# A deformable-convolution kernel: the three parts of a sampling weight row are joined by TensorE, written by ScalarE, and sampling runs in two halves of one PSUM bank

## The reference

```
x = x + attention(norm(x))                    # L0: channel attention, 256 x 256 scores
x = x + dynamic_conv(norm(x))                 # L1: 3x3 kernels made from the image itself
x = x + pointwise(depthwise(norm(x)))         # L2
x = x + dcnv3(norm(x))                        # L3: deformable convolution
# dcnv3: 16 groups of 16 channels, 9 taps a pixel
loc    = pixel + tap + offset                 # offset and mask come from the image
sample = bilinear(in_proj(x), loc)            # four neighbours of each point
out    = out_proj(sum over taps of mask * sample)
```

## Time and profile before

| | us |
|---|---|
| median of 3 runs | 6136.41 (6131.53 to 6136.68) |
| the profiled execution | 6134.27 |
| its span | 6132.4 |
| VectorE busy | 5269.1 |
| TensorE busy (matmul) | 2854.9 |
| ScalarE busy | 1331.2 |
| granted TensorE clock, mean | 0.739 of full speed |

### The profile page before, as it was taken

How to read it: one execution, slowest core, us unless ns; L and a number is a source line. 1 busy time by engine, 2 the same in 40 slices (tenths; PEclk the granted TensorE clock), 3 DMA queues, 4 the chain that set the end, 5 groups by cost and what they waited for, 6 DMA issues and landing times.

```text
span 6132.4 us, 43325 instructions
## 1 busy us (share of the span) xinstructions
PE 2854.9 (47%) x15026; PEld 1623.8 (26%) x15026; DVE 5269.1 (86%) x6291; ACT 1331.2 (22%) x1441; POOL 422.2 (7%) x293
## 2 busy tenths in 40 slices
PE   4442454545345453543545445454544545445233
PEld 2221222223222222322222232222322232232122
DVE  5689899898988989898898989989899898989961
ACT  1311222222122211312221122222212221122210
POOL 0000100001010000100000010000101000010000
PEclk9676676877768777776868678686776878777666
DMA  8101323232322313332241322323232231332253
GB/s 382 50 22 40 99 77 92 69 122 53 91 79 76 113 54 97 99 86 80 68 121 51 91 90 81 101 69 105 71 89 79 77 112 49 96 102 78 83 142 105
DMA packets 619820, 558.08 MB, mean 91 GB/s; under 512 B 463760, under 2 KB 545680, under 8 KB 615632
## 3 DMA queue, kind: packets, MB, share of 16 engines
q1 hardware_dynamic: 615616, 547.85, 29.5%
q0 software_dynamic: 3984, 7.45, 0.5%
HBM read 279.33 MB, written 275.78 MB: 91 GB/s over the span
## 4 chain that ended last, share of the span: by engine, by line
DVE 72%; PE 13%; issue 6%; ACT 5%; POOL 1%; DMA 1%; SPq 1%; DVEq 0%; POOLq 0%; ACTq 0%
DVE spread L1114 9%; DVE partial L1104 9%; DVE spread L1104 6%; DVE qx L776 5%; DVE work L776 5%; DVE partial L1123 5%; DVE partial L1122 5%; DVE work L838 5%; DVE work L829 4%; PE ps L485 4%; PE ps L596 3%; DVE stats L747 2%; PE ps L666 2%; DVE work L889 2%; PE ps L655 1%
## 5 line engine op out<-in xcount | busy, mean ns | idle before, releaser
L553 PE MATMUL ps<-work,w2x 128*128 128x512 f32 x1152 | 558.0, 614 | 174.9 <-DVE work L829 163.8
L1114 DVE TENSOR_TENSOR spread<-spread,partial 128x1344 f32<-128x1344 f32 x384 | 625.2, 1628 | 13.3
L1104 DVE TENSOR_TENSOR partial<-haty,hatx 128x1344 f32<-128x1344 f32 x384 | 596.6, 1554 | 5.6
L1104 DVE TENSOR_TENSOR spread<-haty,hatx 128x1344 f32<-128x1344 f32 x288 | 447.6, 1554 | 77.0 <-ACT qx L1275 64.4
L666 PE MATMUL ps<-samp,wout 128*128 128x256 f32 x1024 | 316.2, 463 | 329.6 <-ACT samp L1347 310.2
L1238 ACT ACTIVATE xp<-x,small 128x1024 f32<-128x1024 f32 x128 | 152.4, 1239 | 1338.4 <-POOL small L1372 1338.4
L485 PE MATMUL ps<-qx,work 128*128 128x512 f32 x512 | 271.6, 690 | 313.1 <-DVE work L855 312.4
L829 DVE SCALAR_TENSOR_TENSOR work<-ps,cols,qx 128x512 f32<-128x512 f32 x576 | 403.2, 746 | 14.3 <-PE ps L553 5.5
L596 PE MATMUL ps<-wts,work 128*128 128x432 f32 x512 | 221.6, 598 | 383.8 <-ACT work L1320 383.8
L485 PE MATMUL ps<-xp,wts 128*128 128x512 f32 x640 | 339.1, 678 | 87.7 <-ACT xp L1238 59.2
L1122 DVE TENSOR_TENSOR partial<-spread 128x576 f32<-128x576 f32 x288 | 344.6, 1196 | 23.0 <-DVE spread L1114 0.4
(11 more groups left out here) (231 smaller groups left out, 4986.2 us busy)
## 6 DMA issues: line engine op xcount, KB each, us to landing
band<-taps_dram SPq DMA_DIRECT2D x512, 384.0 KB
taps_dram<-partial SPq DMA_DIRECT2D x1280, 48.0 KB
near<-img_dram SPq DMA_DIRECT2D x256, 128.0 KB
img_dram<-band SPq DMA_DIRECT2D x6, 4096.0 KB, 40.8
taps_dram<-band SPq DMA_DIRECT2D x6, 4096.0 KB, 86.9
om_now<-om SPq DMA_DIRECT2D x32, 576.0 KB, 9.1
om_dram<-om SPq DMA_DIRECT2D x32, 576.0 KB, 9.6
x<-x_in SPq DMA_DIRECT2D x16, 1024.0 KB, 10.2
```

Source lines behind the costliest of these rows:

```text
L553: pe.matmul(bank(4 + i % 4), w2x[:, half, tap, :], tr[:, h * HALF:(h + 1) * HALF], start=True, stop=True).then_inc(s_w, 1)
L1104: return build(vec.tensor_tensor(o, haty[:, :, 3 * i:3 * i + 3, :].rearrange("p e j a -> p j e a"), cells, ALU.mult))
L1114: done = build(vec.tensor_tensor(skew, skew, spare, ALU.add))
```

## The change

The products and their adds of a unit now go, not skewed, into one of two buffers of `spread`. VectorE starts a unit once the row two back is written (`s_wrow`), and its two joining adds are gone. TensorE adds the three parts in bank 1 by products with the identity: the middle part over 448 columns, the other two over 384 each, shifted against each other. ScalarE writes the row into the ring in two skewed copies: the first and the last vertical distance straight from `spread`, the seven between out of the bank. The ring has two slots, and the wait for a slot's DMAs is now ScalarE's. The steps are `SUM_AT` (1.6 behind the unit's building), 0.2 more for ScalarE and 0.4 more for SP.

A quarter is sampled in two halves of 32 products, both in bank 0. The second half waits until ScalarE has copied the first. There are no zero products any more, but for one at the very start. `SECOND_AT`, `EVICT_AT` and `PROJECT_AT` hold the steps, and the projection of quarter 0 moves from L1 + 4.6 to dyn + 1.5, its result from dyn + 1.1 to dyn + 3.1.

```diff
-RING = 3
+RING = 2
+SUM_AT = [at + 1.6 for at in BUILD_AT]
+TAPS_NEAR = [[i for i in range(3) if abs(u % D - R - (i - 1)) <= REACH] for u in range(UNITS)]
+BUILT = list(accumulate(2 * len(near) - 1 + (u % D == 0) for u, near in enumerate(TAPS_NEAR)))
 SAMPLE_AT = [STEP["L1"] + 1.1, STEP["L2"] + 2, STEP["L3"] + 2, STEP["om"] + 5]
-RESULT_AT = [STEP["dyn"] + 1.1, STEP["pw"], STEP["ln"] - 1, STEP["end"]]
+SECOND_AT = [STEP["L1"] + 6.5, STEP["L2"] + 3, STEP["L3"] + 3, STEP["om"] + 6]
+EVICT_AT = [(STEP["L1"] + 3.5, STEP["L1"] + 8.3), (STEP["L2"] + 3.1, STEP["L2"] + 4.5), (STEP["L3"] + 3.1, STEP["L3"] + 5.2),
+            (STEP["om"] + 5.6, STEP["om"] + 8)]
+PROJECT_AT = [STEP["dyn"] + 1.5, STEP["L2"] + 5.5, STEP["L3"] + 5.6, STEP["om"] + 8.5]
+RESULT_AT = [STEP["dyn"] + 3.1, STEP["pw"], STEP["ln"] - 1, STEP["end"]]
...
-        spread = sb("spread", [P, 3, D, HG])
+        spread = sb("spread", [P, 2, 3, E, HG])
...
-                wait(sp, s_s, 4 * n + quarter)
+                wait(sp, s_s, 2 * (4 * n + quarter))
...
-                    yield at + 4
+                    yield EVICT_AT[quarter][1] + 0.5
...
+            def rows_of_weights(n):
+                for u in range(UNITS):
+                    yield SUM_AT[u]
+                    at = n * UNITS + u
+                    pe.wait_ge(s_wb, n * BUILT[-1] + BUILT[u])
+                    wait(pe, s_wrow, at)
+                    parts = spread[:, at % 2, :, :, :].rearrange("p j e a -> p j (e a)")
+                    inner = (D - 2) * HG
+                    pe.matmul(bank(1, inner), ident, parts[:, 1, :], start=True, stop=False)
+                    pe.matmul(bank(1, inner - HG), ident, parts[:, 0, HG:E * HG], start=False, stop=False)
+                    pe.matmul(bank(1, inner - HG, HG), ident, parts[:, 2, 0:inner - HG], start=False, stop=True).then_inc(s_sum, 1)
...
+                    for part in range(2):
+                        yield (SAMPLE_AT, SECOND_AT)[part][quarter]
+                        wait(pe, s_samp, 2 * at + part)
...
+                    wait(ve, s_wrow, at - 1)
...
-                    done = multiply(near_i[0], skew)
+                    done = multiply(TAPS_NEAR[u][0], total)
...
-                    wait(ve, s_w2[r], 16 * YB * (at // RING))
-                    ve.wait_ge(s_wb, build(vec.tensor_tensor(o, parts[0], parts[1], ALU.add)))
-                    vec.tensor_tensor(o, o, parts[2], ALU.add).then_inc(s_wrow, 1)
-                    ve.wait_ge(s_wrow, at + 1)
...
-                wait(ac, s_wrow, n * UNITS + half * D)
+                wait(ac, s_wb, n * BUILT[-1] + (BUILT[D - 1] if half else 0))
...
+            def rows_of_weights(n):
+                for u in range(UNITS):
+                    yield SUM_AT[u] + 0.2
+                    at = n * UNITS + u
+                    r = at % RING
+                    wait(ac, s_w2[r], 16 * YB * (at // RING))
+                    ac.wait_ge(s_sum, at + 1)
+                    o, parts = ring[:, r, :], spread[:, at % 2, :, :, :]
+                    skew = [[RUN + 1, YI], [YI, G]]
+                    act.activation(bass.AP(o.tensor, o.offset, [list(o.ap[0]), [(D - 1) * RUN, 2]] + skew),
+                                   bass.AP(parts.tensor, parts.offset, [list(parts.ap[0]), [(3 * E - 1) * HG, 2], [G, YI], [1, G]]),
+                                   ACT.Copy)
+                    act.activation(bass.AP(o.tensor, o.offset + RUN, [list(o.ap[0]), [RUN, D - 2]] + skew),
+                                   bank(1, (D - 2) * HG).rearrange("p (d i g) -> p d i g", d=D - 2, i=YI), ACT.Copy).then_inc(s_wrow, 1)
...
+                    for part in range(2):
+                        yield EVICT_AT[quarter][part]
+                        ac.wait_ge(s_s, 2 * at + part + 1)
+                        wait(ac, s_o, at)
+                        act.activation(samp[:, 2 * part:2 * part + 2, :].rearrange("p g (b i x) -> p (g b) i x", b=QB, i=YI),
+                                       bank(0).rearrange("p (b x i) -> p b i x", b=4, i=YI), ACT.Copy).then_inc(s_samp, 1)
```

More of the change, by code:

```diff
@@ L1 @@
 from contextlib import ExitStack
-from itertools import count
+from itertools import accumulate, count
 import concourse.bass as bass
@@ L75, with merged @@
 SAMPLE_AT = [STEP["L1"] + 1.1, STEP["L2"] + 2, STEP["L3"] + 2, STEP["om"] + 5]
[L76 to L77 removed]
+SECOND_AT = [STEP["L1"] + 6.5, STEP["L2"] + 3, STEP["L3"] + 3, STEP["om"] + 6]
[3 more added lines that the diff above has]
+RESULT_AT = [STEP["dyn"] + 3.1, STEP["pw"], STEP["ln"] - 1, STEP["end"]]
+POINTERS_AT, PLACES_AT, VALUES_AT, TURNED_AT, MIXED_AT = (STEP["L0"] + i for i in (1.5, 4.5, 8.5, 9.5, 11.5))
+def merged(*streams):
+    at = [next(stream, END) for stream in streams]
+    while min(at) < END:
+        i = at.index(min(at))
+        yield at[i]
+        at[i] = next(streams[i], END)
 def weave(*streams):
@@ L640, in sample, with taps @@
+            def taps(n):
+                yield from merged(far_points(n), rows_of_weights(n))
             def sample(n):
                 for quarter in range(4):
-                    yield SAMPLE_AT[quarter]
                     at = 4 * n + quarter
-                    wait(pe, s_samp, at)
-                    for b in range(2):
-                        pe.matmul(bank(b), zeros[:, :], cst[:, 0:512], start=True, stop=False, skip_group_check=True)
-                    pe.wait_ge(s_bl, PHASE_LOADS * (at + 1))
@@ L648, in sample @@
-                    for gq in range(4):
-                        for j in range(JB):
-                            a, z = R if j == 0 else 0, SLOTS - R if j == JB - 1 else SLOTS
-                            for s in range(4):
-                                g = 4 * gq + s
-                                o = ps[s * 32:s * 32 + CG, gq // 2, gq % 2 * Q:(gq % 2 + 1) * Q]\
-                                    .rearrange("p (b x i) -> p b x i", b=QB, i=YI)[:, :, j * BW - R + a:j * BW - R + z, :]
-                                mm = pe.matmul(o, near[:, j, g * CG:(g + 1) * CG], band[:, :, j, a:z, g, :],
-                                               start=False, stop=(j == JB - 1), skip_group_check=True)
@@ L657, in sample @@
-                    mm.then_inc(s_s, 1)
-                    yield SAMPLE_AT[quarter] + 3.5
-                    pe.wait_ge(s_samp, at + 1)
+                    for part in range(2):
+                        yield (SAMPLE_AT, SECOND_AT)[part][quarter]
+                        wait(pe, s_samp, 2 * at + part)
+                        if at == 0 and part == 0:
+                            pe.matmul(bank(0), zeros[:, :], cst[:, 0:512], start=True, stop=True)
+                            pe.wait_ge(s_bl, PHASE_LOADS)
+                        elif part == 0:
+                            pe.wait_ge(s_bl, PHASE_LOADS * (at + 1))
+                        for c in range(2):
+                            for j in range(JB):
+                                a, z = R if j == 0 else 0, SLOTS - R if j == JB - 1 else SLOTS
+                                for s in range(4):
+                                    g = 8 * part + 4 * c + s
+                                    o = ps[s * 32:s * 32 + CG, 0, c * Q:(c + 1) * Q]\
+                                        .rearrange("p (b x i) -> p b x i", b=QB, i=YI)[:, :, j * BW - R + a:j * BW - R + z, :]
+                                    mm = pe.matmul(o, near[:, j, g * CG:(g + 1) * CG], band[:, :, j, a:z, g, :],
+                                                   start=(c == 0 and j == 0), stop=(j == JB - 1), skip_group_check=True)
+                        mm.then_inc(s_s, 1)
@@ L1098, in rows_of_weights @@
                         ve.wait_ge(s_hy, 2 * n + half + 1)
-                    near_i = [i for i in range(3) if abs(dx - (i - 1)) <= REACH]
+                    wait(ve, s_wrow, at - 1)
                     def multiply(i, o):
```

38 lines of the change are left out of this document (14 added, 24 removed).

## The result

The changed kernel takes 5758.73 us (median of 4 runs, 5756.81 to 5765.68) where the kernel before takes 6133.97 (4 runs, 6128.7 to 6136.68). The ratio is 0.9391, its 95% interval 0.9375 to 0.9408: faster by 375 us, where 361 were forecast. The profiled execution has a span of 5755.0 us, 377.4 less than before.

The account below looks back on a forecast made before the run. VectorE, busy 86% of the span, was taken as the bound. Terms summed to 23.2 us a period, 348 in 15, plus 13 for the last image: 361 off the span, giving 5775 us, range 5690 to 5890.

Follow-up runs that it names:

- the last kernel: Changed kernel with three sums and one projection moved, the offset stage reordered, five idle products ahead of L1's first products: 5413.7 us, ratio 0.8826 to the kernel before.

## What to carry to other kernels

Work moved from the bound engine to an idle one costs by its place in the queue: an in-order engine that waits for the row holds all that stands behind it, and at such a place the work's own length shows too. Here moving three sums and one projection was worth 203 us, more than half of what the change itself brought. Where VectorE drains banks that TensorE fills, put interruptions singly, and only once TensorE is the one that waits. Before a step is moved into a wait, ask which wait it covers where it stands; and before one wait is shortened, see whether the next one hangs on the same queue.

## What was new about the hardware

- **Skewed writes on ScalarE.** A copy of 448 elements from PSUM to SBUF in steps of 16 bytes took 1020 ns, in one piece 525; 128 elements from SBUF took 433 and 308.
- **TensorE's clock by period.** Periods with the same instructions in the same order met different clocks. With row 6's sum moved, one period in four ran the attention products slower (8.54 against 7.12 us), and periods lasted 332.8, 336.3, 334.4 and 334.5 us in turn; with row 8's sum moved they alternated between 339.2 and 340.1. Gains elsewhere of 0.5 to 2 us a period were in part given back so. What sets the turn wasn't settled. In the last kernel all steady periods were alike.
- **Idle products.** Five products that nobody reads, 2.42 us in a gap of 4.65, shortened the following sixteen records from 10.06 to 8.84 us, though TensorE idled 2.30 us between; that is a period in which VectorE then waited 6.3 us. In the other kind they took 2.95 us, TensorE idled 0.7, the records took 7.16, and VectorE waited 4.8.
